# Cross attention and a mixture-of-experts layer: keys projected in place of queries and values, half-array products, resident gate and up weights, experts unrolled in two halves of the tokens

## What is computed

```
q = layernorm(x) @ Wq[h];  k = c @ Wk[h];  v = c @ Wv[h]           # 8 heads of 128
A = softmax(mask * (q @ k.T) + (1 - mask) * -1e30)                 # 64 x 64 per sequence and head
x1 = layernorm(c + concat_h(A @ v) @ Wo) * gamma0 + beta0
x2 = layernorm(x1 + relu(x1 @ W1 + b1) @ W2 + b2) * gamma1 + beta1
x = x + x2
m = layernorm(x)
s = sigmoid(m @ router_w.T) + bias       # 16 experts in 4 groups; 2 groups, then 4 experts a token
x = x + sum_e w[t, e] * (silu(m @ gate[e]) * (m @ up[e])) @ down[e] + two shared experts, unweighted
```

## Time and profile before

| | |
|---|---|
| median of 3 runs | 342.14 us (341.71 to 342.58) |
| the profiled execution | 341.1 us, its span 339.4 us |
| PE busy | 314.8 us, 93% |
| DVE busy | 220.9 us, 65% |
| ACT busy | 145.5 us, 43% |
| POOL busy | 92.0 us, 27% |
| chain that ended last | PE 76%, DVE 12%, ACT 4% |

### The profile page before, as it was taken

How to read it: one execution, slowest core, us unless ns; L and a number is a source line. 1 busy time by engine, 2 the same in 40 slices (tenths; PEclk the granted TensorE clock), 3 DMA queues, 4 the chain that set the end, 5 groups by cost and what they waited for, 6 DMA issues and landing times.

```text
span 339.4 us, 5140 instructions
## 1 busy us (share of the span) xinstructions
PE 314.8 (93%) x1611; PEld 240.6 (71%) x1611; DVE 220.9 (65%) x568; ACT 145.5 (43%) x266; POOL 92.0 (27%) x105
## 2 busy tenths in 40 slices
PE   3989899999999998986977999999999999999993
PEld 3979789788978896874655666666666666666662
DVE  2818526948895789798676835566566656565654
ACT  2664673477347734662325342333333233333320
POOL 3006413634473444453263042000000000000000
PEclk9999999999999999999997999999999999999999
DMA  8996000000000000002100046333233333323004
GB/s 243 349 272 214 3 0 3 0 0 2 1 3 0 2 0 2 0 4 74 57 0 1 2 138 240 124 116 106 95 118 124 124 124 124 122 114 102 32 0 124
DMA packets 18773, 26.79 MB, mean 79 GB/s; under 512 B 1330, under 2 KB 13124, under 8 KB 18628
## 3 DMA queue, kind: packets, MB, share of 16 engines
q1 hardware_dynamic: 16676, 25.52, 22.8%
q10 hardware_dynamic: 2080, 1.05, 1.1%
HBM read 25.38 MB, written 1.18 MB: 78 GB/s over the span
## 4 chain that ended last, share of the span: by engine, by line
PE 76%; DVE 12%; ACT 4%; issue 3%; POOL 2%; DMA 1%; DVEq 0%; POOLq 0%; ACTq 0%
PE bank L1331 17%; PE bank L1059 12%; PE bank L1061 12%; PE bank L1060 12%; PE bank L1144 8%; PE bank L1122 7%; DVE cen L725 3%; PE bank L1171 2%; DVE sc_m L768 2%; ACT prob_T L525 2%; PE bank L1201 1%; DMA wqk_in<-in_L_xattn_Wq 1%; ACT v_o L510 1%; DVE stat L709 1%; ACT hid L535 1%
## 5 line engine op out<-in xcount | busy, mean ns | idle before, releaser
L646 ACT ACTIVATE wT<-bank 128x512 f32<-128x512 f32 x72 | 43.0, 597 | 84.9 <-PE bank L1061 84.8
L1059 PE MATMUL bank<-mT_hi,we_hi 128*128 128x512 f32 x128 | 74.0, 578 | 3.9 <-DVE wT L992 2.0
L992 DVE TENSOR_TENSOR wT<-bank,wT 128x512 f32<-128x512 f32 x64 | 44.1, 691 | 39.5 <-PE bank L1061 29.8
L1061 PE MATMUL bank<-mT_hi,we_lo 128*128 128x512 f32 x128 | 50.5, 394 | 0.0
L1060 PE MATMUL bank<-mT_lo,we_hi 128*128 128x512 f32 x128 | 50.3, 393 | 0.0
L1059 PEld LDWEIGHTS bank<-mT_hi,we_hi 128*128 128x128 f32 x128 | 24.0, 188 | 22.0 <-issue 12.3
L398 POOL TENSOR_TENSOR we_lo<-w_exp,we_hi 128x256 fp32r<-128x256 f32 x16 | 11.8, 740 | 97.8 <-ACT we_hi L567 97.8
L1331 PE MATMUL bank<-wT,we_dn 128*128 128x512 f32 x72 | 37.5, 605 | 0.0
L1331 PE MATMUL bank<-q_T,we_dn 128*128 128x512 f32 x72 | 36.5, 592 | 0.0
L1060 PEld LDWEIGHTS bank<-mT_lo,we_hi 128*128 128x128 f32 x128 | 24.1, 188 | 16.7 <-issue 14.0
L1122 PEld LDWEIGHTS bank<-cT_m,q_T 128*128 128x128 f32 x256 | 30.3, 192 | 6.4 <-DVE sc_m L768 5.9
(11 more groups left out here) (181 smaller groups left out, 529.9 us busy)
## 6 DMA issues: line engine op xcount, KB each, us to landing
wvo_in<-comb_dram SPq DMA_DIRECT2D x16, 512.0 KB, 3.5
wqk_in<-comb_dram SPq DMA_DIRECT2D x15, 512.0 KB, 3.6
mask_row<-in_mask_BxS_ff SPq DMA_DIRECT2D x1, 1024.0 KB, 8.8
out_x<-ctx_all SPq DMA_DIRECT2D x4, 256.0 KB, 2.8
x_all<-in_x SPq DMA_DIRECT2D x1, 768.0 KB, 8.2
ctx_all<-in_ctx SPq DMA_DIRECT2D x1, 768.0 KB, 10.5
wqk_in<-in_L_xattn_Wq ACTq DMA_DIRECT2D x1, 512.0 KB, 4.8
wqk_in<-in_L_xattn_Wk ACTq DMA_DIRECT2D x1, 512.0 KB, 5.6
```

The costliest lines, as they stand in the source:

```text
L646: a.activation(silu[k % 2], h_bank[k % 2][:], ACT.Silu).then_inc(silu_ready, 1)
L992: v.tensor_tensor(s_u[k % 2], u_bank[k % 2][:], silu[k % 2], ALU.mult).then_inc(s_u_ready, 1)
L1059: pe.matmul(dst, w_hi, m_hi, start=start, stop=False)
L1061: return pe.matmul(dst, w_lo, m_hi, start=False, stop=stop)
```

## The change

**Layout.** The host only rearranges the inputs (`layout`): tiles side by side, weights in pairs (wq, wk) and (wv, wo), gate and up side by side, the small vectors in one row. The turns of the weights on PE are gone: `fold` multiplies what the DMA brings. The context comes a second time with its partition halves swapped (`ctx_swap`), the mask as a column and per pair.

**Attention.** Keys are projected through the folded weights (`key`, eight per chunk, one chunk ahead, two per pair) in place of queries. There is no `values`: probabilities multiply the raw context (`attend`, four f32 products of 256 columns over 64 rows), ACT copies the result (`heads_out`, two copies), and `project` multiplies it with `vo`. `scores` is two f32 products with 64 stationary columns, each into one half of the PSUM partitions. `spread` is one copy. ACT applies the norms 1 and 3. POOL masks the context. The loop runs over 16 pairs, and `attend` and `project` are one and two pairs behind `scores`.

**Experts.** All gate and up weights are split during attention (pairs of experts after pairs 3, 4, 5, 7, 8, 9, 11, 12, 13) and stay in SBUF. The 72 steps are written out: first chunks 0 and 1 for all experts, then chunks 2 and 3. Weights of the tokens come in a ring of four. DVE does all weighing, one step behind `gate_up`. Chunks 0 and 1 leave during the second half.

```diff
-            for i, ready in enumerate((ld_wq, ld_wk, ld_wv)):
-                pe.wait_ge(ready, 16)
-                for half in range(2):
-                    for h in range(HP):
-                        src = wqk_in[:, i, half * HP + h, :] if i < 2 else wv_in[:, half * HP + h, :]
-                        last = pe.transpose(bank[2 * i + half][:, h * P:(h + 1) * P], src, ident[:])
-                    last.then_inc(w_turned, 1)
...
+            def fold(i, half):
+                pe.wait_ge(ld_w[i][half], 16)
+                a, b = (1, 0) if i == 0 else (0, 1)
+                for h in range(HP):
+                    last = pe.matmul(fold_bank[2 * i + half][:, h * P:(h + 1) * P], w_in[:, i, half, h, a, :],
+                                     w_in[:, i, half, h, b, :], start=True, stop=True)
+                last.then_inc(fold_done, 1)
...
+            def key(c, h):
+                i = h % 2
...
+                if i == 1 and c:
+                    pe.wait_ge(sc_taken, (c - 1) * TPC + h // 2 + 1)
+                three(key_bank[i][:], qk_hi[:, h, :], qk_lo[:, h, :], cT_hi[:], cT_lo[:], True, True
+                      ).then_inc(key_full[i], 1)
...
+            def scores(n):
...
+                for s in range(2):
+                    b = 2 * p + s
+                    tok = n * P + s * SEQ
+                    pe.matmul(sc_bank[s * SEQ:(s + 1) * SEQ, :], xnT[:, tok:tok + SEQ],
+                              k_T[c % 2][:, b, :, :].rearrange("p h t -> p (h t)"), start=True, stop=True
+                              ).then_inc(sc_full, 1)
...
+            def attend(n):
+                pe.wait_ge(prob_T_ready, n + 1)
+                if n:
+                    for j in range(2):
+                        pe.wait_ge(o_taken[j], n)
+                for s in range(2):
+                    for j in range(2):
+                        rows = slice(j * SEQ, (j + 1) * SEQ)
+                        held = ctx_all if s == j else ctx_swap
+                        last = pe.matmul(o_bank[j][:].rearrange("p (h b s) -> p h b s", b=2, s=SEQ)[:, :, s, :],
+                                         held[rows, n, :], prob_T[n % 2][rows, :, s, :], start=True, stop=True)
+                        if s == 1:
+                            last.then_inc(o_full[j], 1)
+            def project(n):
+                for j in range(2):
+                    pe.wait_ge(o_taken[j], n + 1)
...
+                for h in range(NH):
+                    last = pe.matmul(av_bank[:, 0:P], o_T[n % 2][:, h % 2, h // 2, :], vo[:, h, :],
+                                     start=(h == 0), stop=(h == NH - 1))
+                last.then_inc(av_full, 1)
...
+            for m in range(NT):
+                c, p = divmod(m, TPC)
+                ahead = c + 1 < CH
+                scores(m)
+                if ahead:
+                    key(c + 1, 2 * p)
...
+                if p == 0 and c >= 2:
+                    ffn_down(c - 2)
+                if p == 3 and c >= 1:
+                    turn_x1(c - 1)
+                if ahead:
+                    key(c + 1, 2 * p + 1)
...
+                if p == 2 and c >= 2:
+                    turn_xm(c - 2)
+                if p == 3 and c + 2 < CH:
+                    turn_ctx(c + 2)
+                if p == 3 and c >= 1:
...
+                    ffn_up(c - 1, 0)
+                if m >= 1:
+                    turn_probs(m - 1)
...
+                if m >= 2:
+                    project(m - 2)
...
+                if m >= 1:
+                    attend(m - 1)
+                if p == 2 and c >= 2:
...
+                    route(c - 2)
+                if p == 3 and c >= 1:
+                    ffn_up(c - 1, 1)
+
+            ffn_down(CH - 2)
+            turn_probs(NT - 1)
+            project(NT - 2)
+            attend(NT - 1)
...
+            up(0)
+            pe.wait_ge(logits_ready, 2)
+            up(1)
+            project(NT - 1)
+            for n in range(2, N):
+                if n == 2:
+                    turn_combine(0)
+                if n == 4:
+                    turn_xm(CH - 2)
...
+                up(n)
+                if n >= LAG:
+                    down(n - LAG)
...
+            for m in range(NT):
...
+                if ahead:
+                    key(c + 1, 2 * p)
...
+                if p == 2 and c >= 2:
+                    normalise(3, c - 2, tokens(x2, c - 2))
+                if p == 3 and c >= 1:
+                    normalise(1, c - 1, tokens(y, c - 1))
+                    turn_x1(c - 1)
+                exponent(m)
+                if ahead:
+                    key(c + 1, 2 * p + 1)
...
+                if p == 2 and c >= 2:
+                    xm_high(c - 2)
+                if p == 3 and c + 2 < CH:
+                    cT_high(c + 2)
+                if p == 3 and c >= 1:
+                    hidden(c - 1, 0)
+                if m >= 1:
+                    spread(m - 1)
+                    heads_out(m - 1)
+                if p == 3 and c >= 1:
+                    hidden(c - 1, 1)
+                if m in SPLITS:
+                    split_hi(SPLITS.index(m))
+            router_sigmoid(0)
+            spread(NT - 1)
+            heads_out(NT - 1)
...
+            add_ctx(NT - 3)
+            bias_scores(0)
+            add_ffn(CH - 2)
+            statistics(2, CH - 2, z)
+            group_scores(0)
+            keep_groups(0)
+            add_ctx(NT - 2)
+            residual(CH - 2)
+            keep_experts(0)
+            statistics(3, CH - 2, tokens(x2, CH - 2))
+            combine(0)
+            for n in range(N):
+                gate_up(n)
+                if n and weighted(n - 1):
+                    weigh(n - 1)
+                if n == 0:
+                    add_ctx(NT - 1)
+                    v.wait_ge(y_ready, NT)
+                    statistics(1, CH - 1, tokens(y, CH - 1))
+                if n == 1:
+                    take_combine(0)
...
+        def order(a, b):
+            first = [(e, c) for c in (a, b) for e in range(NSH)]
+            last = [(e, c) for c in (a, b) for e in (NX - 2, NX - 1)]
+            return first + [(e, c) for e in range(NSH, NX - 2) for c in (a, b)] + last
+        STEPS = order(0, 1) + order(2, 3)
```

More of the change, by code:

```diff
@@ L51, with build @@
 LAG = 4
[L52 to L57, removed]
+RING = 4
+GU = 2 * P
+VEC = 4 + P + NE
+def build(nc, x, ctx_in, mask_tok, mask_pairs, w_attn, w_gu, w_dn, small, w1, w2, vec, out):
     es = ExitStack()
     with es:
-        es.enter_context(nc.allow_non_contiguous_dma(reason="two small vectors"))
         def sb(name, shape, dt=F32):
@@ L98, in build @@
[L98 to L106, removed]
+        k_T = [sb(f"k_T{i}", [P, BPC, NH, SEQ]) for i in range(2)]
@@ L518, in spread @@
-            def spread(c, p):
-                a.wait_ge(t_full, c * TPC + (p + 1))
-                if not (c == 0 and p < 2):
-                    a.wait_ge(av_full, c * TPC + (p - 1))
-                for s in range(2):
-                    rows = slice(s * SEQ, (s + 1) * SEQ)
-                    last = a.copy(prob_T[p % 2][rows, :, s, :],
-                                  t_bank[rows, :].rearrange("p (h s) -> p h s", s=SEQ))
-                last.then_inc(prob_T_ready, 1)
+                    for h in range(NH - 2, NH):
+                        a.wait_ge(key_full[h % 2], key_use(c - 1, h))
@@ L913, in take_combine @@
                 v.tensor_copy(comb_T[0:rows, b, :], comb_bank[b][0:rows, 0:P]).then_inc(comb_T_ready, 1)
[L916 to L933 removed]
+            for m in range(NT):
+                c, p = divmod(m, TPC)
+                if m >= 3:
+                    add_ctx(m - 3)
+                mask_and_max(m)
+                if c == 0 and p + 1 < CH:
+                    if p < 2:
+                        v.wait_ge((ld_x1, ld_x)[p], 16)
+                    statistics(0, p + 1, tokens(x_all, p + 1))
+                if p == 1 and c >= 2:
@@ L947, in _ @@
-                mask_and_max(c, 0)
-                if last:
-                    v.wait_ge(y_ready, c * TPC)
-                    statistics(1, c - 1, tokens(y, c - 1))
-                if before:
+                sum_of_exp(m)
+                if c == 0 and p + 1 < CH:
+                    normalise(0, p + 1, tokens(x_all, p + 1))
+                if p == 0 and c >= 2:
+                    add_ffn(c - 2)
+                    statistics(2, c - 2, z)
+                if p == 1 and c >= 2:
+                    statistics(3, c - 2, tokens(x2, c - 2))
@@ L1106, in three_moving @@
[L1106 to L1116 removed]
+                if c:
+                    pe.wait_ge(key_free[0], ctx_use(c) - 1)
```

1265 lines of the change are left out of this document (519 added, 746 removed).

## The result

The changed kernel takes 342.7 us (median of 20 runs, 341.09 to 344.12) against 341.89 us before (20 runs, 340.83 to 342.58): ratio 1.0029, 95% interval 1.0016 to 1.0041, 0.3% slower. The forecast was 336. The profiled execution took 344.12 us for a span of 342.4, so it stands 1.4 us above the median of its kernel.

A forecast was written before the change was run, and what follows sets the result against it. PE's own work was taken as the bound. Stretches of 16.3, 123.8 and 193.0 gave a 333.1 us span; adding 1.7 and 1.0 gave 335.8, rounded 336. Range 331 to 340 for its own case, 323 to 352 with rivals.

The forecast's parts named there:

- Experts, 72 x 2.247: Expert steps on PE: still 72 steps of the same seven products, 161.8 us before and after.
- First scores at 16.3: Kernel start: without the weight turns and their copies, first scores come at 16.3 instead of 22.5 us, gain 6.2.
- The halves: Attention's half-array products overlap partly: scores 1.29 plus 0.16 us for changing modes, attend 1.07 a pair; chance 0.50.
- side by side in full: Rival for scores and attend: halves overlap fully, 0.86 + 0.16 and 0.87 us a pair, total 326; chance 0.15.
- Plain pairs, 7.1 us with 0.7 of stall: Attention pairs without extra chunk work: 0.16 + 1.29 + 4.57 + 1.07 us, including 0.7 of PE stall on the softmax chain.
- the loop, 123.8 us: Attention loop over 16 pairs: 138.7 us with halves one after the other, less 0.93 a pair.
- the special pairs: Loop pairs with extra chunk work; before the 0.93 reduction, pairs 7, 10, 11, 13, 14 were 11.8, 10.3, 11.4, 7.5, 9.6 us.
- Theory B: Stated with the follow-up runs, not the prediction: the softmax chain itself is so long, whatever the engines' order; no chance given.
- The seam, 193.0: From the loop's end to the kernel's end: last attention work, routing, experts and output, 193.0 us.
- The stall ahead of step 2: Behind the loop, PE waits some 7.7 us for DVE's routing, mainly at turn_combine(0).
- the seam eats it: Rival: the stall behind the loop drops the clock, 4 us of work become 8, total 342; chance 0.10.

The follow-up runs named there:

- Run 7: Changed kernel plus 18 turns of the identity on PE, read by nothing, while the first weights come: 341.41 us, ratio 0.9998.
- run 2: Changed kernel with attend's four products issued half 0, half 0, half 1, half 1 instead of alternating: 343.24 us, ratio 1.0047.
- run 14: Changed kernel with all four attend products reading rows 0 to 63, same amount of work: 352.55 us, ratio 1.0309.
- run 1: Changed kernel with POOL's split_lo issued behind the next pair's subtraction instead of ahead of it: 340.76 us, ratio 0.9974.
- slots: Changed kernel with normalise(1) a pair earlier on ACT, normalise(3) on DVE, turn_x1 and turn_xm in the next pair on PE: 338.22 us alone, ratio 0.9868.
- run 12: Changed kernel with the slots, split_lo behind the next subtraction and add_beta one pair later, without PE fillers: 329.2 us, ratio 0.9643.
- run 13: Changed kernel with only unread or repeated PE products added inside its waits (identity turns, project repeated): 339.18 us, ratio 0.9928.
- run 10: Changed kernel with the slots, split_lo and add_beta moved later, identity turns before the first weights, project(15) three times: 327.99 us, ratio 0.9615.

## Why the prediction was wrong

The span is 9.3 us over the forecast (342.4 against 333.1): 1.7 ahead of the first scores, 7.5 in the loop, 0.1 behind it.

**Experts, 72 x 2.247: right.** Steps still start 2.25 us apart from 226.5 us on (2.7 the two with an output turn between them), and PE waits for no weighing.

**First scores at 16.3: 18.00 measured.** The first key came at 10.04, not 9.5. Fold's first four products took 1.85 us from their start to the turn behind them, at the half pace that I had priced (1.8); but that turn took 0.85 where I had 0.44, and the sum that says "with a wake each" holds no wake. The other 1.2 us lie behind: keys waited in pairs for their two banks (starts at 10.04, 11.65, 13.38, where two keys are 1.39 us of PE), and ACT's copies of those banks were not in the sum. Run 7, which only keeps PE busy ahead of the fold, had the first key at 9.20 and the scores at 16.75.

**The halves: 1.29 + 0.16 us forecast for scores, 1.01 measured; 1.07 for attend, 1.06 measured.** The reason was wrong in both: not "the second record of one can lie beside the first of the next, and no more", for the group takes 1.07 us in either order (run 2), and 1.92 only when both use the same rows (run 14). The rival "side by side in full" had the mechanism. What the groups take above its 0.86 and 0.87 lies at their ends: from attend's last record to the scores 0.31 us where its records stand 0.216 apart, from the scores' last record to the key 0.52 where such records stand 0.43 apart. That is 0.09 us at each change, so the 0.16 a pair that I had put for it is about right in size, and that attend met its forecast is luck. The Trainium skill ("TensorE: Matmul & The Clock Gate", Part 3) says that products in different row groups run concurrently. The traces agree: the first records of both halves start at 57.92.

**Plain pairs, 7.1 us with 0.7 of stall: right in number (6.97, stall 0.70), by luck.** The scores were 0.44 us cheaper than forecast, and `split_lo` ahead of the subtraction, at nothing in the sum, took most of it back (6.5 to 6.6 in run 1).

**The step that failed is the loop, 123.8 us against 131.3**, and in it the special pairs. Pairs 7, 10, 11, 13 and 14 were summed at 10.9, 9.4, 10.5, 6.6 and 8.7 (46.0) and took 54.5; all others together took 1.0 less than forecast. I had ACT's normalise ahead of the exponent in the sum, but nothing of the order on the other engines: `split_lo` (nine times 1.3 us) was costed at nothing though it is issued ahead of the subtraction on the critical chain, `add_beta` and the roots as well (the roots were moved in no run), and PE's position at `turn_x1` and `turn_xm` while ACT normalises was not checked. Some 2.8 of the 7.5 us belong to this execution: run 2's, whose edit only changes the order within `attend`, has a loop of 128.5 us, with pair 2 at 6.44 and pair 7 at 11.12 us behind the same waits, and there the five pairs take 53.0. The sizes: orders on POOL and slots together 13.5 us (342.7 to 329.2, run 12). A part of it is the clock that falls with the waits: run 13, which changes no order, gains 3.5, of which 1.3 stand ahead of the loop (run 7). With the orders mended the five pairs take 41.3 us in run 12, 4.7 less than forecast, and the loop of run 10 goes from 16.78 to 133.2, 116.4 us, 7 less than I forecast for it: the cheaper halves were there all along. Theory B falls: the chain was not long whatever the order. How much of the slots' part is order and how much normalise(3) on DVE stays open.

**The seam, 193.0: right in its sum** (149.3 to 342.4), by luck. The stall ahead of step 2 was 4.7, not 7.7 us; nine products of steps 2 and 3 then ran at half pace (0.43 us each instead of 0.23), and 1.6 us were lost at the second `turn_combine`.

**The clock** was a rival only ("the seam eats it", 342), and only at the seam. It went down in six slices. What it does to one pair shows in pair 2, `attend` and `scores`, in the profiled execution of the changed kernel and then in that of run 2:

```profile
29.21 0.45 PE L1045 MATMUL bank<-prob_T,ctx_all 64*128 64x256 f32 x1 [2.09 <-ACT prob_T L534]
...
30.27 1.97 PE L1022 MATMUL bank<-k_T,xnT 128*64 128x512 f32 x4
```

```profile
29.17 0.45 PE L1045 MATMUL bank<-prob_T,ctx_all 64*128 64x256 f32 x1 [2.10 <-ACT prob_T L534]
...
30.24 1.08 PE L1022 MATMUL bank<-k_T,xnT 128*64 128x512 f32 x4
```

The wait is the same, and only in the first are the products behind it at half pace. The mean granted clock of an execution goes with its time, but loosely: in the changed kernel 0.963 goes with 343.8 to 344.1 us and 0.978 with 341.9 to 342.0, but 0.973 with 341.1 to 343.6 and 0.979 with 342.6; in run 1 0.963 goes with 342.9 to 343.6 and 0.977 with 338.7 to 339.1.

## What to carry to other kernels

When PE gets shorter and the chain beside it sets the pace, price every engine by its issue order: for each operation that is new or moved, ask what the next link of the critical chain finds ahead of it, on GpSimd's queue too. A wait that was harmless can be followed by products at half pace, so its price is the wait and what the products behind it lose. And don't judge such an edit alone: the single repairs that gained anything gave 1.3 to 4.5 us here, three others lost 1 to 7, and the best together gave 14.7. Nor judge by one profile: two executions with the same waits differed by 2.8 us in the loop.

## What was not expected of the hardware

An f32 product over 64 rows runs beside one over the other 64 rows also when two of the first half are issued ahead of both of the second (1.07 us in both orders, 1.92 on the same rows). Two f32 products of 512 columns into the two halves of the PSUM partitions run side by side too: four records in 1.01 us, where they stand 0.43 apart elsewhere.

The same wait doesn't always cost the same: behind 2.1 us in pair 2 and 2.2 us in pair 7 PE ran at half pace in one execution and at its full pace in another. There the clock made the difference and not a longer wait; what decides whether it falls no run here shows. In run 1 0.014 of the mean granted clock were 4 us; by my estimate a mean lower by 0.014 over 340 us is 9.5 us at 1.2 GHz, in which 4.8 us of work are not done, so in that run most of it lay on the path.

At the start the granted clock is no guide to the pace: fold's first eight records stand 0.23 us apart where such records take 0.112 later, and the profile's page gives 9 for that slice.
